# Decoder layer on one core: spreading of the context values waits for the cross queries, with four smaller moves of work

## The reference

```python
x = layernorm(x + self_attention(x))          # 16 heads of 64
x = layernorm(x + cross_attention(x, ctx))    # 16 heads of 64, softmax over the heads of one token
x = layernorm(x + ffn(x))                     # light and heavy expert
```

```python
scores = jnp.einsum('bshd,bsgd->bshg', q, k) * inv_sqrt_dk
attn = jax.nn.softmax(scores, axis=-1)
out = jnp.einsum('bshg,bsgd->bshd', attn, v)
out = jnp.transpose(out, (0, 2, 1, 3)).reshape(b, -1, N_HEADS * D_K)
```

## Time and profile before

| what | us |
|---|---|
| median of 3 runs (399.01 to 399.64) | 399.55 |
| the profiled execution | 399.96 |
| its span in the profile | 398.1 |
| TensorE busy (matmul) | 386.8 |
| VectorE busy | 286.6 |
| ScalarE busy | 240.0 |
| POOL busy | 146.8 |

### The profile page before, as it was taken

The page is one execution under the profiler, slowest core; times in us unless marked ns, Lnnn a source line. Parts: engine busy times, 40 slices in busy tenths (PEclk is TensorE's granted clock), DMA queues, the critical chain, the costliest instruction groups (busy, mean ns, idle before and its releaser), DMA issues.

```text
span 398.1 us, 16460 instructions
## 1 busy us (share of the span) xinstructions
PE 386.8 (97%) x6836; PEld 335.9 (84%) x6836; DVE 286.6 (72%) x661; ACT 240.0 (60%) x815; POOL 146.8 (37%) x223
## 2 busy tenths in 40 slices
PE   8999899999999999999999999999999999899995
PEld 8797788888898888888988888878988888788985
DVE  4586797965849688776848778777848878687555
ACT  5585675845666485735568465745667566456451
POOL 0540544431513454421414454422415445323214
PEclk9999999999999999999999999999999999999999
DMA  7910112310110213110100213100101111211001
GB/s 233 374 47 8 40 31 47 85 38 2 36 29 12 53 24 93 36 28 8 36 21 20 44 33 91 37 21 8 36 22 27 43 37 22 49 39 25 28 27 54
DMA packets 43760, 19.37 MB, mean 49 GB/s; under 512 B 36592, under 2 KB 41200, under 8 KB 43696
## 3 DMA queue, kind: packets, MB, share of 16 engines
q1 hardware_dynamic: 42880, 16.88, 16.4%
q0 software_dynamic: 528, 1.45, 1.0%
q10 hardware_dynamic: 288, 0.07, 0.1%
HBM read 8.95 MB, written 1.05 MB: 25 GB/s over the span
## 4 chain that ended last, share of the span: by engine, by line
PE 89%; DVE 3%; ACT 2%; DMA 2%; SPq 1%; issue 1%; POOL 1%; POOLq 0%; DVEq 0%
PE ps L1254 8%; PE ps L1104 8%; PE ps L1199 7%; PE ps L1076 7%; PE ps L1167 7%; PE ps L1179 7%; PE ps L1056 5%; PE ps L1156 5%; PE ps L1058 4%; PE ps L1057 4%; PE ps L1095 4%; PE ps L1209 4%; PE ps L1132 3%; PE ps L1193 2%; PE ps L1187 2%; PE ps L1195 2%
## 5 line engine op out<-in xcount | busy, mean ns | idle before, releaser
L559 ACT ACTIVATE p<-ps,neg_max 128x128 f32<-128x128 f32 x256 | 90.0, 382 | 38.4 <-DVE neg_max L829 38.3
L409 POOL TENSOR_TENSOR p<-p,row_inv 128x1024 f32<-128x1024 f32 x32 | 60.7, 1897 | 63.9 <-DVE row_inv L835 63.9
L552 ACT ACTIVATE pt<-ps 128x512 f32<-128x512 f32 x62 | 34.0, 614 | 46.6 <-PE ps L1156 46.3
L559 ACT ACTIVATION_READ_ACCUMULATOR p<-ps,neg_max 128x1 f32 x256 | 57.4, 224 | 0.0
L829 DVE TENSOR_REDUCE neg_max<-ps 128x4 f32<-128x512 f32 x64 | 41.6, 674 | 4.9 <-PE ps L1254 4.0
L775 DVE TENSOR_TENSOR ot<-ps,bv 128x512 f32<-128x512 f32 x32 | 22.0, 689 | 25.5 <-PE ps L1179 25.3
L1167 PE MATMUL ps<-x1t,wq 128*64 128x64 f32 x1024 | 34.3, 224 | 1.1 <-issue 0.7
L1254 PE MATMUL ps<-kt,qt 64*64 64x128 f32 x1024 | 35.2, 275 | 0.0
L1167 PEld LDWEIGHTS ps<-x1t,wq 128*64 128x64 f32 x1024 | 31.7, 138 | 2.7 <-issue 1.6
L1104 PE MATMUL ps<-wo,ot 128*128 128x128 f32 x256 | 32.3, 279 | 1.5 <-DVE ot L721 1.5
L1199 PE MATMUL ps<-wo,ot 128*128 128x128 f32 x256 | 32.7, 281 | 0.3 <-DVE ot L775 0.3
(11 more groups left out here) (158 smaller groups left out, 828.8 us busy)
## 6 DMA issues: line engine op xcount, KB each, us to landing
v<-v2s SPq DMA_DIRECT2D x256, 32.0 KB
xg<-x_t SPq DMA_DIRECT2D x4, 256.0 KB, 2.6
cg<-ctx_t SPq DMA_DIRECT2D x4, 256.0 KB, 2.8
wo<-w_o SPq DMA_DIRECT2D x2, 512.0 KB, 9.8
xres<-x_nat SPq DMA_DIRECT2D x15, 64.0 KB, 1.8
pt<-w_qk SPq DMA_DIRECT2D x3, 256.0 KB, 4.8
out<-x2b SPq DMA_DIRECT2D x3, 256.0 KB, 2.3
x2b<-w_v SPq DMA_DIRECT2D x1, 512.0 KB, 7.8
```

The source lines that it names most:

```text
L409: nc.gpsimd.tensor_tensor(ph, ph, row_inv[:, 8 * half:8 * half + 8].unsqueeze(2).to_broadcast([T, 8, T]), ALU.mult).then_inc(p_ready, 1)
L559: last = nc.scalar.activation(p[:, hd * T:(hd + 1) * T], bank(S_BANK[q])[:, pos * T:(pos + 1) * T], ACT.Exp, bias=neg_max[:, hd:hd + 1], a ...
```

## The change

Five edits. SP's spreading has one more wait, for both halves of the cross queries of the same step. In step 0, VectorE and ScalarE evict block B before they split the last 512 columns of the query and key weights. In step 0, TensorE projects units 0 and 1 of block F, transposes the first half of p, and then projects units 2 and 3. In step 15, VectorE regroups before it evicts the cross queries, as in phases 0 to 2. And `wup_lo` is computed by POOL, at the end of its step 2, and no more by VectorE.

```diff
--- before.py
+++ after.py
@@ -315,6 +315,8 @@
 
                     sp.wait_ge(mm_pv2, 2 * s - 2)
                 sp.wait_ge(v2s_ready, 2 * s)
+
+                sp.wait_ge(mm_q2, 2 * s)
                 for pp in range(2):
                     for j in range(J):
                         for ih in range(IH):
@@ -433,6 +435,9 @@
                     rstd2(s)
                 if bc:
                     minus_max2(s + 1)
+                if isinstance(s, int) and s == 2:
+                    pool.wait_ge(wup_split, 1)
+                    nc.gpsimd.tensor_tensor(wup_lo[:], wup, wup_hi[:].bitcast(fp32), ALU.subtract).then_inc(wup_split, 1)
                 if isinstance(s, int) and s == 1:
 
                     pool.wait_ge(in_ffn, 7 * 16)
@@ -574,8 +579,8 @@
                     split_hi(3)
                     act.wait_ge(bq_scaled, 1)
                     qk_out(0, "A", FIRST_BANKS)
+                    qk_out(0, "B")
                     split_hi(4)
-                    qk_out(0, "B")
                 projecting = phase < 2 and a
                 if bc:
                     transposed(2)
@@ -915,13 +920,14 @@
                 if bc:
                     if static and s == 1:
                         dve.wait_ge(in_own_j, 16)
-                    if d and phase < 3:
+                    queries_first = phase == 3 and not (static and s == B - 1)
+                    if d and not queries_first:
                         regrouped(s)
                     q2_out(s, 0)
                     if static and s == 1:
                         inverse_sums(1)
                     q2_out(s, 1)
-                    if d and phase == 3:
+                    if d and queries_first:
                         regrouped(s)
                 if phase == 0 and a and bc:
                     c_low(g)
@@ -943,9 +949,6 @@
                     dve.wait_ge(in_ffn, 7 * 16)
                     nc.vector.tensor_scalar(wup[:, 0:FH], wup[:, 0:FH], gam[:, 1:2], D ** 0.5, ALU.mult, ALU.mult).then_inc(wup_scaled, 1)
                     nc.vector.tensor_scalar(wup[:, FH:FP], wup[:, FH:FP], gam[:, 0:1], D ** 0.5, ALU.mult, ALU.mult).then_inc(wup_scaled, 1)
-                if static and s == 2:
-                    dve.wait_ge(wup_split, 1)
-                    nc.vector.tensor_tensor(wup_lo[:], wup, wup_hi[:].bitcast(fp32), ALU.subtract).then_inc(wup_split, 1)
 
             run_steps(dve, step)
 
@@ -1369,7 +1372,7 @@
                     pe.wait_ge(exp_ready, 2)
                     pe.wait_ge(w_lo, WV_SPLIT)
                     values(0)
-                    project_k2(0, "F", lambda r: read_k2(r, "E"))
+                    project_k2(0, "F", lambda r: read_k2(r, "E"), units=(0, 1))
                     pe.wait_ge(in_ident, 16)
 
                     pe.wait_ge(v_ready, 2)
@@ -1378,6 +1381,9 @@
 
                         pe.wait_ge(xnt_ready, s - 2)
                     transpose_p(s, 0)
+                if static and s == 0:
+
+                    project_k2(0, "F", lambda r: read_k2(r, "E"), units=(2, 3))
                 if phase == 3 and not static:
                     pe.wait_ge(x_lo, g + 2)
```

## The result

| | before | after |
|---|---|---|
| median of 5 runs | 399.55 (399.01 to 400.43) | 401.75 (401.38 to 402.10) |
| the profiled execution | 399.96 | 402.10 |
| its span | 398.1 | 400.2 |
| TensorE busy | 386.8 | 387.3 |

The ratio is 1.0063 (95% interval 1.0040 to 1.0085): the change makes the kernel slower, by 2.2 us in the medians. That is well under 2% and yet clear of the noise of these runs. The forecast was 400.2 us with a range up to 401.4.

The account below looks back on a forecast made before the run. TensorE, busy 97% of the span, was taken as the bound, so only its idle time counted. Terms -0.30 - 0.67 - 0.26 + 0.5 + 1.4 + 0 = +0.67 us gave 400.2 us against the 399.55 median; range 398.2 to 401.4.

Parts of the forecast that it names:

- edit 2: Step 0, block F: TensorE transposes the first half of p between units; its 0.67 us wait goes: -0.67, ends -0.67 and 0.
- edit 1: Step 0: block B evicted before the split of the last weights; TensorE's 0.36 us idle goes: -0.30, ends -0.36 and 0.
- edit 3: POOL instead of VectorE makes wup_lo; TensorE's 0.26 us wait at 67.80 goes: -0.26, ends -0.26 and 0.
- edits 4 and 5, step 15: Regrouping first plus the later spreading: VectorE held before v2s, 0.5 us reaching TensorE: +0.5, ends -0.64 and +2.2.
- edit 5, last weighting: Tail: the last spreading waits for step 16's cross queries, so TensorE waits 1.4 us for v2: +1.4, ends 0 and +3.1.
- ordinary steps, issue stalls: Later spreadings cost nothing in ordinary steps; eight TensorE stalls, 2.4 us together, stay: 0, stalls' ends 0 and -2.4.
- 11.2 us in all: Length of a spreading, from first issue at 127.81 to no packet left at 139.0; 10.10 us of it is issuing.
- Edit 4: Step 15: VectorE regroups before evicting the cross queries; 0.64 us comes off TensorE's 1.51 wait, but is lost before v2s.
- edit 5: Every spreading waits for the cross queries' end, 1.3 to 1.7 us later; free in ordinary steps, costly in the tail.
- Rival C: Slower: one of the last two spreadings takes 11.78 us, lengthening the tail's wait; 1.7 more, 401.9 us; chance 0.2.
- Rival B: Tail waits don't bite, as the last spreadings are issued or land quicker; sum -1.87, 397.7 us; chance 0.12.
- rival D: The change is inert: SP finds the queries already done; 398 to 399.6 us by the other edits; chance 0.03.

## Why the prediction was wrong

**The mechanism was right, two sizes were not.** Every sign of the forecast was there: idle time at 12, 31 and 67 us gone, some 0.9 us (0.75) left before `project_o2`, nearly 2 us (1.84) of VectorE's wait before v2s, a wait for v2 before the last weighting, none in ordinary steps, and the stalls still there. But both waits in the tail were longer than priced, and edit 2 gave less:

| term | forecast | measured |
|---|---|---|
| edit 1 | −0.30 | −0.37 |
| edit 2 | −0.67 | −0.46 |
| edit 3 | −0.26 | −0.31 |
| edits 4 and 5, step 15 | +0.5 | +0.75 |
| edit 5, last weighting | +1.4 | +1.70 |
| ordinary steps, issue stalls | 0 | 0 |
| sum | +0.67 | +1.31 |

**The step that failed: "11.2 us in all".** I took the length of a spreading from packets: none was left 11.2 us after the first issue. From there came "+0.5" and "+1.4", measured as +0.75 and +1.70. What holds an engine is not the packet but the release behind it. In the kernel after, VectorE started v2s at 350.75, 11.45 us behind the first issue at 339.30, and TensorE the last weighting at 370.51, 11.46 us behind 359.05. The last packets of the tail's spreading lie in this stretch (DMA queues, 370.1 to 370.2):

```profile
q1 hardware_dynamic: 4, 0.00, 3.9%
```

Four begin there and none later, and 3.9% of 16 engines for 0.1 us is 0.06 us for all four; so they are over by 370.2, and 0.3 us or more passed between the last packet and the release. That is the 0.25 missing in step 15. At the last weighting the same 0.26 is missing, and 0.13 more on the way to SP's first issue, 3.28 us behind the first weighting's start where I had 3.15; against that, my 359.1 plus 11.2 is 370.3 and I had written 370.4. The Trainium skill, DMA: Bandwidth & Descriptors, on the fixed cost of a transfer, gives about 2.0 us, most of it behind the last byte; its breakdown is for transfers issued by GpSimd, and SP issues these. The trace agrees with the size: the sixteenth issue began near 368.5 (359.05 plus fifteen times 0.63), 2.0 us before TensorE went on. It does not agree with the split. Of the tail's spreading, issued from 359.05, no packet runs in the stretch 359.0 to 360.2, and 45 begin in 360.2 to 360.4 (DMA packets, then the queue):

```profile
DMA packets 0, 0.00 MB, mean 0 GB/s; under 512 B 0, under 2 KB 0, under 8 KB 0
...
q1 hardware_dynamic: 45, 0.01, 25.1%
```

So some 1.2 us lie ahead of a transfer's first packet and only 0.3 to 0.4 behind the last. I had put the page's rule at 0.35 us more for each wait and 400.9, and left it out of the sum; 0.25 to 0.3 were measured.

The forecast stood 0.15 us below the bound of what can be told, so two waits longer by 0.3 us were enough to take it over that bound: with the measured terms the same working gives 400.84. That is still inside the range. What took the time out of it is the further 0.9 us of the first measurement, which no term holds (below); measured again, beside its variants, the change took 400.90.

**Edit 2** freed its idle time, but took something back. Before, block F, both halves of p and the wait lasted 5.53 us, from 25.18 to 30.71; after, the four pieces follow each other without idle time from 25.31 to 30.39, 5.08. Without its wait of 0.67 the first would be 4.86: cutting the work in four costs TensorE 0.22 us with no wait in the rows (from start to next start, block F took 3.80 us in two pieces for 3.64 in one, and the transposes 1.28 for 1.22). I had put the two more changes of operation at nothing, without a reason.

**Edit 1** was worth its whole idle time: the split of the last weights, now later, held nothing. **Edit 3** hid as foreseen, though `wup_lo` took POOL 1.55 us, not 1.26 (POOL's timeline of the kernel after):

```profile
64.70 0.62 POOL L375 TENSOR_TENSOR s<-s,mx 128x256 f32<-128x256 f32 x1 [1.90 <-DVE mx L730]
65.28 1.55 POOL L440 TENSOR_TENSOR wup_lo<-x2b,wup_hi 128x640 fp32r<-128x640 f32 x1
67.20 0.62 POOL L380 TENSOR_TENSOR p<-s,inv 128x256 f32<-128x256 f32 x1 [0.37 <-DVE inv L738]
```

The subtraction beside it fell from the 1.13 us of the earlier trace rows to 0.62, and behind `wup_lo` POOL stood idle 0.37 us for the input of its next work, so nothing waited for it. **Edit 4** was lost in edit 5's wait, as said, and the reason holds further than I saw: even without the wait step 15's spreading bounds that stretch.

**Rival C was the nearest,** slower through a longer wait in the tail, but with the wrong cause: neither of the last two spreadings took 11.78 us to issue (10.09 and 10.08). Longer ones there were, in ordinary steps, where they had room (SP's timeline of the kernel after, steps 2 and 7):

```profile
58.44 12.02 SPq L325 DMA_DIRECT2D v<-v2s  x16
...
163.97 12.34 SPq L325 DMA_DIRECT2D v<-v2s  x16
```

The first of them was a near miss, which I had not looked for: its last issue ended at 70.46, so that by the tail's 1.4 us from there to a release it was over near 71.8, and VectorE wrote v2s next at 72.15. Rival C's 401.9 lies 0.15 us above the time, and I cut the range at 401.4, before it. **Rival B** fell with both waits, **rival D** with the 2.44 us that the wait alone costs.

**What stays open.** The terms give +1.31 us, the medians +2.2 (interval 1.6 to 3.4) and, for the same kernel again, +1.65 (1.0 to 2.9). The second holds the sum, the first does not quite. In the other experiments the terms come within 0.35 us of the medians' differences, but for the change without the wait, which is 0.7 us faster than its terms. These two gaps may lie where profiles of the same code differ, in the start (first product at 5.48 to 6.21 us) and in the stalls of steps 3 to 15, by up to 2.1 us. That is not shown: no run separates these from some small effect of the change. The wait in the ordinary steps showed none in the one run made for it. The sign does not hang on it: the wait alone gave +2.44 us for terms of 0.77 + 1.71, and the change without it −2.44.

## What to carry to other kernels

Before moving a transfer's start, list who waits for its end, and look at the last step or two by themselves: the ordinary steps had room for every spreading, if only some 0.3 us behind step 2, and no wait for one showed there, while the tail, where the work between start and use runs out, paid for each tenth. Price such a wait from the first issue to an engine's restart, not to the last packet, and if a few tenths of a microsecond decide the sign, let the range and the chances say so. And a gain on an engine that is about to wait for a transfer is no gain: of edit 4's 0.59 us nothing was left.

## What the runs showed of the hardware

- The queue "instruction" moved 54 packets of 16 KB in the kernel after. They go with TensorE (6,836 products and as many weight loads are some 250 instructions for each), and idle time put down to "issue", 0.2 to 0.9 us, stands behind some of them. In steps 3 to 15 of the twelve profiles it ends 1.2 to 2.4 us behind the packet, at one of the same eight products, and appears or not from one execution to the next. Two profiles of the same code differed by 2.1 us over these steps, more than most edits here were worth.
- From the start of a spreading's last issue to the engine that waited for it lay 2.0 us; from its last packet, 0.3 to 0.4; and from its first issue to its first packet, 1.2.
- Cutting a run of 64 products (block F) in two and putting 16 transposes between cost TensorE 0.22 us without any wait.
